# Moving value loads, expert numbers, a gather's index row and one weight wait in a fused cross-attention and mixture-of-experts kernel

## What is computed

```python
x = x + xattn(layernorm(x), ctx)      # 16 heads, 77 context rows
x = x + ffn(layernorm(x))

def ffn(x):                           # 8 experts, the best two per token
    probs = softmax(x @ Wg + bg)
    top_v, top_i = top_k(probs, 2)
    top_v = top_v / (top_v.sum(-1) + 1e-6)
    for e in range(8):
        h = silu(x @ W1[e] + b1[e]) * (x @ W3[e] + b3[e])
        out += combine[:, e] * (h @ W2[e] + b2[e])
```

## Time and profile before

| | |
|---|---|
| three timed runs | 158.48, 159.10, 159.77 us, median 159.1 |
| the profiled execution | 157.44 us |
| its span, first to last instruction | 155.5 us, so 1.9 us lie around it |
| granted TensorE clock, mean of the span | 1.000 |
| busy: PE, DVE, POOL, ACT | 142.5, 103.0, 80.9, 78.9 us |

### The profile page before, as it was taken

One profiled execution on the slowest core, in us unless ns is written; L12 is line 12 of the kernel. 1 busy time (PEld: TensorE's weight loads), 2 busy tenths in 40 slices (PEclk: granted clock), 3 DMA queues, 4 the chain that ended last, 5 costly groups with the idle time before them and its releaser, 6 DMA issues.

```text
span 155.5 us, 4064 instructions
## 1 busy us (share of the span) xinstructions
PE 142.5 (92%) x1208; PEld 134.7 (87%) x1208; DVE 103.0 (66%) x318; ACT 78.9 (51%) x222; POOL 80.9 (52%) x98
## 2 busy tenths in 40 slices
PE   5988897889999999988599979999999999999991
PEld 5977785769989999987489978999999999999991
DVE  0546599998899986886887984636536355385441
ACT  3088365874647486760155523345476453544131
POOL 3550001958625678210678057777777777776000
PEclk9999999999999999999999999999999999999999
DMA  4999998212000000325946766687969887821343
GB/s 139 329 323 290 248 132 93 50 52 87 2 2 0 4 0 21 114 72 158 288 145 213 235 203 189 189 220 242 237 111 386 245 252 223 256 79 55 113 173 135
DMA packets 20013, 24.50 MB, mean 158 GB/s; under 512 B 3085, under 2 KB 11625, under 8 KB 19993
## 3 DMA queue, kind: packets, MB, share of 16 engines
q1 hardware_dynamic: 17952, 20.57, 47.8%
q0 software_dynamic: 1440, 2.82, 6.2%
q10 hardware_dynamic: 601, 0.87, 1.5%
HBM read 19.91 MB, written 4.33 MB: 156 GB/s over the span
## 4 chain that ended last, share of the span: by engine, by line
PE 71%; DVE 11%; ACT 8%; DMA 4%; issue 2%; DVEq 1%; ACTq 0%
PE psum L1395 24%; PE psum L1408 13%; PE psum L1456 9%; PE psum L1438 5%; PE psum L1169 2%; PE psum L1422 2%; PE psum L1171 2%; PE psum L1170 2%; DMA ctx_sb<-in_ctx_dram 2%; DMA g_room<-xf_scratch,idx 2%; DVE prob L848 2%; DVE negmax L843 2%; PE psum L1203 2%; ACT g_room L642 2%; PE psum L1380 2%
## 5 line engine op out<-in xcount | busy, mean ns | idle before, releaser
L1395 PE MATMUL psum<-probT,w 128*128 128x128 f32 x368 | 45.3, 276 | 0.4 <-ACT probT L731 0.3
L1395 PEld LDWEIGHTS psum<-probT,w 128*128 128x128 f32 x368 | 43.0, 192 | 0.7 <-ACT probT L731 0.7
L742 ACT ACTIVATE prob<-psum,bias_col 128x128 f32<-128x128 f32 x92 | 26.2, 368 | 32.1 <-PE psum L1395 30.6
L1104 DVE SCALAR_TENSOR_TENSOR probT<-psum,bias_col,prob 128x128 f32<-128x128 f32 x92 | 26.0, 345 | 23.9 <-ACT prob L742 23.7
L572 POOL DMA_INDIRECT g_room<-xf_scratch,idx x22 | 22.1, 1003 | 18.3 <-DVE idx L1087 6.8
L528 POOL TENSOR_TENSOR prob<-prob,rowsum 128x1232 f32<-128x1232 f32 x8 | 18.0, 2249 | 23.2 <-DVE rowsum L839 23.2
L1408 PE MATMUL psum<-w,probT 128*128 x184 | 24.7, 278 | 0.4 <-DVE probT L1104 0.4
L1408 PEld LDWEIGHTS psum<-w,probT 128*128 128x128 f32 x184 | 22.4, 191 | 0.7 <-issue 0.5
L1456 PE MATMUL psum<-vo,probT 128*128 128x128 f32 (+1 forms) x160 | 19.3, 276 | 0.0
L581 POOL DMA_INDIRECT y_scratch<-xnT,out_row x16 | 16.3, 1020 | 5.5 <-issue 4.3
L1456 PEld LDWEIGHTS psum<-vo,probT 128*128 128x128 f32 (+1 forms) x160 | 18.5, 192 | 0.0
(11 more groups left out here) (183 smaller groups left out, 203.2 us busy)
## 6 DMA issues: line engine op xcount, KB each, us to landing
w<-in_L_ffn_W_dram SPq DMA_DIRECT2D x54, 256.0 KB, 5.4
early<-in_L_xattn_W_kv_dram SPq DMA_DIRECT2D x2, 512.0 KB, 6.1
y_scratch<-zero_rows SPq DMA_DIRECT2D x2, 512.0 KB
x_sb<-in_x_dram SPq DMA_DIRECT2D x2, 256.0 KB, 4.8
early<-in_L_xattn_W_q_dram SPq DMA_DIRECT2D x1, 512.0 KB, 6.0
early<-in_L_xattn_W_out_dram SPq DMA_DIRECT2D x1, 512.0 KB, 8.4
early<-in_L_ffn_b_dram SPq DMA_DIRECT2D x1, 512.0 KB, 3.9
xf_scratch<-xf SPq DMA_DIRECT2D x2, 256.0 KB, 2.2
```

The source lines that it names most:

```text
L742: act.activation(silu[:, j % 2, c, :], psum[:, 2 * (j % 2), c * P:(c + 1) * P], ACT.Silu, bias=bias_col[:, 0, bass.ds(expert, 1), c]).then ...
L1104: dve.scalar_tensor_tensor(out=hT[:, j % 2, c, :], in0=psum[:, 2 * (j % 2) + 1, c * P:(c + 1) * P], scalar=bias_col[:, 1, bass.ds(expert[j ...
L1395: ins = pe.matmul(psum[:, 2 * (j % 2) + a, c * P:(c + 1) * P], w13[:, j % WR, a, c * P:(c + 1) * P], xt[:, j % XR, :], start=True, stop=True)
```

## The change

Five edits. (1) The two `load_expert` on VectorE between `first_tiles` and the first `idx` go; tile 0's load now stands ahead of `shifts(2)`, those of tiles 1 and 2 behind `blocks_of(2)`. (2) `other_experts`, which makes `eid` of tiles 5 to 22, moves from VectorE to GpSimd, ahead of the sixth gather (`gather(5)`), as eight instructions with a semaphore wait between them in place of five. (3) `last_powers` moves from ahead of gather 5 to behind it. (4) `other_rows` moves from behind `gated(2)` to ahead of it, and `bias_down(0)` from ahead of `gated(2)` to ahead of `gated(1)`. (5) SyncE waits for gather 5 to land before it reads the expert of tile 7 and issues that tile's weights.

```diff
             for j in range(WR, NT):
                 if j == FULL:
                     sp.wait_ge(eid_ok, 1)
+                elif j == FULL + 2:
+                    sp.wait_ge(xg_ok[FULL], 16)
                 elif j == 2 * FULL + 4:
...
+            def other_experts():
+
+                pool.wait_ge(base_ok, 1)
+                pool.tensor_tensor(end_e[:, :], base[0:1, :], padded[0:1, :], ALU.add).then_inc(p_eid, 1)
+                pool.wait_ge(p_eid, 1)
+                pool.tensor_tensor(end_e[:, :], end_e[:, :], taken_e[0:1, :], ALU.add).then_inc(p_eid, 1)
+                pool.wait_ge(p_eid, 2)
+                pool.tensor_tensor(ended[:, :, :], iota_j[0:1, FULL:NT].rearrange("p (j o) -> p j o", o=1).broadcast_to([1, NT - FULL, E]),
+                                   end_e[:, :].rearrange("p (o e) -> p o e", o=1).broadcast_to([1, NT - FULL, E]),
+                                   ALU.subtract).then_inc(p_eid, 1)
+                pool.wait_ge(p_eid, 3)
+                pool.tensor_scalar(ended[:, :, :], ended[:, :, :], 0.0, None, ALU.is_ge).then_inc(p_eid, 1)
+                pool.wait_ge(p_eid, 4)
+                for n, half in enumerate((4, 2)):
+                    pool.tensor_tensor(ended[:, :, 0:half], ended[:, :, 0:half], ended[:, :, half:2 * half], ALU.add).then_inc(p_eid, 1)
+                    pool.wait_ge(p_eid, 5 + n)
+                pool.tensor_tensor(eid_f[:, FULL:NT], ended[:, :, 0], ended[:, :, 1], ALU.add).then_inc(p_eid, 1)
+                pool.wait_ge(p_eid, 7)
+                pool.tensor_scalar(eid[:, FULL:NT], eid_f[:, FULL:NT], float(E - 1), None, ALU.min).then_inc(eid_ok, 1)
...
                 if j == FULL:
+                    other_experts()
+                elif j == FULL + 1:
                     last_powers()
                 gather(j)
...
-                link(dve.tensor_reduce(base[:, :], low_pad[:, :, :], AX.X, ALU.add))
+                dve.tensor_reduce(base[:, :], low_pad[:, :, :], AX.X, ALU.add).then_inc(base_ok, 1)
+                dve.wait_ge(base_ok, 1)
...
             first_tiles()
-            load_expert(0)
-            load_expert(1)
             dve.wait_ge(idx_1_mm, 1)
             dve.tensor_scalar(idx[:, 0:FULL], FIRST_AT, row_base[:, 0:1], None, ALU.add).then_inc(idx_1_ok, 1)
             first_one_hots()
             add_direct(6)
             add_direct(7)
             taken_blocks()
+            load_expert(0)
             shifts(2)
             top_two(2)
...
             gated(0)
             other_bases()
-            other_experts()
-            load_expert(2)
             ranks(2)
             blocks_of(2)
+            load_expert(1)
+            load_expert(2)
+            dve.wait_ge(ld["bias"], 16)
+            bias_down(0)
             gated(1)
             other_tiles()
             one_hots(2)
-            dve.wait_ge(ld["bias"], 16)
-            bias_down(0)
+            other_rows()
             gated(2)
-            other_rows()
             bias_down(1)
```

More of the change, by code:

```diff
@@ L280, in build @@
         base_e_ok = sem("base_e_ok")
+        base_ok = sem("base_ok")
+        p_eid = sem("p_eid")
         expo_ok = sem("expo_ok")
@@ L1019, in other_tiles @@
                                   ALU.mult).then_inc(hit_ok, 1)
[L1021 to L1028, removed]
             def other_rows():
```

## The result

The changed kernel takes 160.28 us (median of four runs, 159.67 to 160.97) against 158.79 before (median of four, 156.82 to 159.77). The ratio is 1.0167 with a 95% interval of 1.0119 to 1.0215: slower. It is not the ratio of these two medians: 160.28 / 1.0167 is 157.65 us, the mean of the two shortest of the four runs before. All ten of these executions have a mean granted clock of 0.989; so have 21 of the 60 of the kernel before that ran beside the experiments (158.85 us or more; all but one are left out of the ratios, and what lowered their clock was not profiled), and none of the 81 of e1 to e3 and e6 to e11, where the loads stand elsewhere.

The account below looks back on a forecast made before the run. TensorE's chain, set by the second dispatch's first tiles, was taken as the bound. Tile 5's 1.28 us gain, given back with 0.6 on top at tile 6, made 159.1 + 0.6 = 159.7 us, range 158.2 to 161.2.

Parts of the forecast that it names:

- the base of 159.1: Median of the three timed runs before, to which 0.6 us was added; the profiled execution lay 1.7 below it.
- The front: First dispatch without its two loads: first index row 1.11 us earlier, one load idling VectorE 0.65, up(1) 0.75 earlier.
- VectorE: VectorE up to the second index row: gated(1) 1.1 us earlier, the row 1.5 earlier, tile 5's transpose 1.28 earlier.
- The expert numbers on GpSimd: Eight dependent instructions ahead of gather 5 take 3.1 us, hidden in GpSimd's idle time and costed at nothing.
- The power and gather 6: Power of 3.33 us ahead of gather 6: issue at 93.75, landing 3.4 us, tile 6's transpose 0.6 us later than before.
- The first gather's 4.9: Rival: gather 6 lands in 4.9 us behind two tiles' weights, tile 6 2.1 later, 161.2 us, slower; chance 0.15.
- The estimate of 2.15 us: The skill's landing time for a gather's 64 KB: tile 6 0.65 early, 158.45 us; no weight beyond the empty-queue rival's 0.13.
- the sum: Tile 5's 1.28 us gain is given back with 0.6 on top at tile 6; no later tile waits.
- The end: GpSimd's last scatters: 0.25 us at most is left for the end, costed at nothing.
- The hold: Tile 7's weights wait for gather 5's landing; needed only at up(7), eight us after issue, so it costs nothing.

Follow-up runs that it names:

- e1: The changed kernel with the power moved between the expert numbers and gather 5; ratio 0.9888 to the kernel before, 155.51 us.
- e3: The changed kernel without SyncE's wait for gather 5 ahead of tile 7's weights; ratio 1.0099 to the kernel before, 158.97 us.
- e6: The kernel before with only the loads moved out of the first dispatch, to where the change puts them; ratio 1.0021, 157.82 us.
- e11: e1 with tile 2's load moved to the idle time ahead of the second index row; ratio 0.9885 to the kernel before, 155.52 us.
- e8: e1 with the expert numbers back on VectorE; ratio 0.9976 to the kernel before, 157.20 us.
- e2: The changed kernel with 20 unused filler transposes on TensorE ahead of tile 6's transpose; ratio 1.0084 to the kernel before, 158.74 us.
- e7: e1 without SyncE's wait for gather 5 ahead of tile 7's weights; ratio 0.9986 to the kernel before, 157.31 us.
- e4: The kernel before with only the power moved behind gather 5; ratio 1.0183, 160.09 us.
- e5: The changed kernel run again on another chip, with no edit; ratio 1.0176 to the kernel before, 160.08 us.

## Why the prediction was wrong

The forecast was 159.7 us, 0.6 us or 0.4% above the median before, with 0.79 on a change within 1%; measured were 1.67%, or 2.63 us (160.28 less 157.65). That the measured time lies inside the range, 0.6 us from the forecast, is luck: the forecast change was 2.0 us too small and the base of 159.1 was 1.45 too high. Two of the three runs behind that base (159.10 and 159.77) lie where the kernel before, in the runs beside the experiments, has a granted clock of 0.989; the profiled execution, 157.44 us at a clock of 1.00, would have been the better base. The steps of the forecast, each against its place since the first `slot_rows`:

- **The front held.** The first index row gained 1.05 us (1.11 forecast). The load cost 0.95 of idle time instead of 0.65, but `up(1)` gained 0.81 (0.75).
- **VectorE held roughly.** Two loads took 1.49, 0.2 more than forecast, and `gated(1)` gained 0.62 instead of 1.1. `slot_rows`, which TensorE sets as well, gained 0.62 (0.75), the second index row 1.40 (1.5), gather 5 1.41 (1.5), tile 5 1.27 (1.28). That the last agrees so well is luck too: `up(4)` gained 0.13 where 0.3 was forecast, and the transpose followed its start by 1.79 us instead of the 1.93 counted.
- **The expert numbers on GpSimd** took 2.98 us (3.1) and lay in idle time. "GPSIMD Engine Reference" of the Trainium skill, Engine selection, puts two-input elementwise work on VectorE, GpSimd being about half as fast; 1.2 us there against 2.98 here agrees with its direction, though here they are eight instructions with waits between them instead of five. e8 shows that the move pays 0.9 us all the same, because VectorE is waited for and GpSimd is not.
- **The power and gather 6.** Gather 6 went out where it was forecast (21.13 against 21.06). It landed in 3.9 us, where 3.4 had been taken, and tile 6 was 1.18 late instead of 0.6. So this term was mis-sized by half a microsecond. The first gather's 4.9, the rival that I had for slower, did not happen (nor was it the longest of the kernel before: the gather of 117.56 took 5.0). The estimate of 2.15 us by "DMA: Bandwidth & Descriptors" of the Trainium skill, Anatomy of one DMA, was further off: 3.9 here, and 2.5 or more wherever a landing was read.
- **The step that failed is the sum**, where it says that no later tile waits and lets each tile take its 2.8 us. That pace is the pace at a granted clock of 1.00, and I carried it across a wait that I had myself put at about 1.9 us. Behind the wait of 2.48 the clock was at its lower level, and tiles 6 to 7 took 4.50 us instead of 2.79: 1.71 us that no term of the sum and no rival contained. "TensorE: Matmul & The Clock Gate" of the Trainium skill, HAM oscillation — how this bites in real kernels, says that a wait for a DMA can send the matmuls behind it back to the slow clock; the trace agrees (0.52 behind the wait, 1.00 ahead of it), and e2 shows it on the time: with TensorE kept busy through the same wait, 1.6 us come back.
- **The end held:** from tile 7 on, both spans need the same time (56.1 and 56.2 us).

Together: 1.18 of waiting and 1.71 of clock make 2.9 us at tile 7. The profiled spans differ by 3.7 (159.2 less 155.5), which is this and the 0.74 ahead of the change that differs from execution to execution; the runs differ by 2.63.

The hold was taken for free and harmless. It was more: with it gather 5 landed in time, without it (e7) the loss was 1.3 us. And it is no gain everywhere: in the changed kernel tile 7 came 0.8 us earlier without it (e3), where the waiting was split in two and the clock stayed up. The rows that the forecast rested on had shown the gathers next to weights at 3.2 and 4.1, but I asked only what the held weights would do to gather 6.

## What to carry to other kernels

Where an engine runs in order, a long instruction belongs in front of the wait that follows, not behind it: GpSimd idled 4.4 us ahead of gather 5, and the same 2.95 us of power cost nothing there, and one place later they cost 4.4 us at tile 7 (29.58 against 25.21 in e1), 1.7 of them through the clock. When a change puts a wait on TensorE, price the matmuls behind it at the lower clock too, and keep it busy through the wait if the wait can't go. A gain early in a chain is only worth what the next engine down the chain can take: the loads alone won 1 us at the first dispatch and nothing at the end.

## What the runs showed of the hardware

A wait of TensorE of 2.48 us in one profile and of 2.57 in another was followed by the lower clock, and all ten executions of that kernel have a mean clock of 0.989; waits of 0.82 and 2.02 us (e3), or of 0.99 and 1.40 (e4), were not followed by it in their profiles. What decides between them is not shown. The lower level came 1.2 us behind the wait in one profile and right behind it in the other, and cost 1.7 and 1.8 us. One scalar read by VectorE left 0.48 us of idle time or 0.95 in the instruction stream, two in a row 1.5. An indirect gather of 128 rows landed after 2.5 to 5.0 us; gather 5 landed after 2.7 with tile 7's weights held back (e5), and without the hold after 4.0 and 4.1 (e3, e7) or 2.93 (before).
